# Attention over 48 pairs: one phase of transposes and one of scores per pair, on four shared PSUM banks

## What is computed

```
x + xattn(ctx_1024, layernorm(x), mask, g1, b1, g2, b2, Wq, Wkv, Wout)

xn = layer_norm(ctx, g1, b1)                 # (2, 2048, 512)
ln = layer_norm(latents, g2, b2)             # (2, 128, 512), the latents
q  = ln @ Wq                                 # 16 heads of 64
k, v = split(concat([xn, ln], 1) @ Wkv)
weight = einsum('bhld,bhnd->bhln', q * scale, k * scale)
weight = softmax(where(full_mask, weight, neg), -1)
out = einsum('bhln,bhnd->bhld', weight, v) @ Wout
```

## Time and profile before

| | |
|---|---|
| median of 3 runs | 971.02 us (970.89 to 972.89) |
| the profiled execution | 970.6 us, its span 968.8 us |
| TensorE (PE) busy | 881.1 us, 91% of the span |
| VectorE (DVE) busy | 612.3 us, 63% |
| ScalarE (ACT) busy | 489.1 us, 50% |
| GpSimd (POOL) busy | 313.6 us, 32% |
| the chain that ended last | PE 76%, DVE 12%, ACT 5% |
| the pair loop | from about 52 to 675 us |

### The profile page before, as it was taken

How to read it: one execution, slowest core, us unless ns; L and a number is a source line. 1 busy time by engine, 2 the same in 40 slices (tenths; PEclk the granted TensorE clock), 3 DMA queues, 4 the chain that set the end, 5 groups by cost and what they waited for, 6 DMA issues and landing times.

```text
span 968.8 us, 17165 instructions
## 1 busy us (share of the span) xinstructions
PE 881.1 (91%) x6217; PEld 796.1 (82%) x6217; DVE 612.3 (63%) x1550; ACT 489.1 (50%) x1051; POOL 313.6 (32%) x284
## 2 busy tenths in 40 slices
PE   3799999999999999999999999998686687978997
PEld 2699999999998999999999999887464586867885
DVE  6445556665667776565666566666386377865785
ACT  3465564545555554445464554554557253543553
POOL 3642623120121313131312000220726367744443
PEclk9799999999999999999999999999797888989999
DMA  6255413131323232322212222324220522321320
GB/s 191 59 193 185 157 56 119 66 125 66 111 82 124 87 130 106 124 88 99 83 65 98 87 87 83 124 93 154 95 86 1 190 82 93 131 87 66 110 88 23
DMA packets 45219, 99.13 MB, mean 102 GB/s; under 512 B 3744, under 2 KB 16976, under 8 KB 41936
## 3 DMA queue, kind: packets, MB, share of 16 engines
q1 hardware_dynamic: 45040, 98.00, 29.6%
q10 hardware_dynamic: 96, 0.02, 0.0%
HBM read 88.06 MB, written 8.91 MB: 100 GB/s over the span
## 4 chain that ended last, share of the span: by engine, by line
PE 76%; DVE 12%; ACT 5%; issue 3%; POOL 3%; DMA 1%; DVEq 0%; SPq 0%; ACTq 0%
PE pJ L1620 15%; PE pJ L1622 13%; PE pJ L1621 13%; PE pV L1761 7%; PE pS L1737 7%; PE pT L1747 6%; POOL WS L578 2%; PE pS L1620 2%; DVE KV L1109 2%; PE pS L1621 2%; PE pS L1622 2%; PE pX L1660 1%; DVE late L1577 1%; PE pV L1620 1%; DVE st L1122 1%
## 5 line engine op out<-in xcount | busy, mean ns | idle before, releaser
L1620 PE MATMUL pJ<-WV,XT 128*128 128x256 f32 x544 | 162.9, 300 | 0.0
L1622 PE MATMUL pJ<-WV,XT 128*128 128x256 f32 x544 | 154.3, 284 | 0.0
L1621 PE MATMUL pJ<-WV,XT 128*128 128x256 f32 x544 | 154.2, 284 | 0.0
L1620 PE MATMUL pJ<-XT,WK 128*128 128x384 f32 (+1 forms) x384 | 130.2, 339 | 4.5 <-POOL XT L601 2.6
L1622 PE MATMUL pJ<-XT,WK 128*128 128x384 f32 (+1 forms) x384 | 126.0, 328 | 0.0
L1621 PE MATMUL pJ<-XT,WK 128*128 128x384 f32 (+1 forms) x384 | 125.7, 327 | 0.0
L601 POOL TENSOR_TENSOR XT<-xtmp,XT 128x384 fp32r<-128x384 f32 (+1 forms) x44 | 41.3, 939 | 244.7 <-ACT XT L767 244.4
L842 ACT ACTIVATE PT<-pT 128x384 fp32r<-128x384 f32 x192 | 80.2, 473 | 70.3 <-PE pT L1747 70.3
L1620 PEld LDWEIGHTS pJ<-WV,XT 128*128 128x128 f32 x544 | 104.3, 192 | 10.0 <-issue 8.0
L1109 DVE TENSOR_TENSOR PT<-pT,PT 128x384 fp32r<-128x384 f32 x192 | 95.9, 527 | 18.9 <-ACT PT L842 18.7
L1621 PEld LDWEIGHTS pJ<-WV,XT 128*128 128x128 f32 x544 | 104.4, 192 | 0.0
(11 more groups left out here) (338 smaller groups left out, 2126.2 us busy)
## 6 DMA issues: line engine op xcount, KB each, us to landing
WV<-wv_split SPq DMA_DIRECT2D x20, 1024.0 KB, 4.9
WK<-wk_split SPq DMA_DIRECT2D x40, 512.0 KB, 3.5
xraw<-in_ctx SPq DMA_DIRECT2D x7, 768.0 KB, 4.7
wk_split<-WK SPq DMA_DIRECT2D x8, 512.0 KB, 3.6
wv_split<-WV SPq DMA_DIRECT2D x4, 1024.0 KB, 6.8
wst<-in_L_ffn_Wg SPq DMA_DIRECT2D x4, 1024.0 KB, 5.1
raw<-in_L_ffn_Wu SPq DMA_DIRECT2D x4, 1024.0 KB, 5.1
work<-in_L_ffn_Wd SPq DMA_DIRECT2D x4, 1024.0 KB, 5.3
```

Of the source, the lines that this page charges most:

```text
L1620: te.matmul(dst, a(HI), b(HI), start=start, stop=False)
L1621: te.matmul(dst, a(HI), b(LO), start=False, stop=False)
L1622: return te.matmul(dst, a(LO), b(HI), start=False, stop=stop)
```

## The change

The two phases of transposes of a pair become one at its start, followed by rows_of_scales; the scores of both halves stand side by side behind the value tiles and use the banks of the transposes (BANK: the two of pS and the two of pT), so scores(n, q) wait for the low halves of pair I's probabilities. PT gets a fourth slot (PT3). Keys are projected for pair I + 2, after the outputs, and the third value tiles come behind them. The lists of the other engines follow: key_hi and key_lo move to the end of a pair, joined_hi, value_lo, mask_bias and stats change their places among them, loads, stores and splits of the keys' weights are one pair earlier, and waits that say that a round's context is used up (`after_round`) take its values in.

```diff
             scl = xb("scl", [P, 2, 2, L])
+            PT3 = xb("PT3", [P, 2, CWID], F32R)
...
         ROWS = (slice(0, DH), slice(DH, P))
+        BANK = (pS[:, 0, :], pS[:, 1, :], pT[:, 0, :], pT[:, 1, :])
+        PTS = (PT[:, 0], PT[:, 1], PT[:, 2], PT3)
         pO = pV[:, :].rearrange("p (h s t) -> p h s t", h=2, s=2)
...
-        jobs = ["Q0", "K0.0", "V0.0", "K0.1", "V0.1", "V0.2", "Q1"]
+        jobs = ["Q0", "K0.0", "V0.0", "K0.1", "V0.1", "V0.2", "Q1", "K1.0", "K1.1"]
         for I in range(ITERS):
-            if I + 1 < ITERS:
-                jobs += [f"K{I + 1}.0", f"K{I + 1}.1"]
             if I // 2 + 1 < GROUPS:
                 jobs += [f"V{I // 2 + 1}.{I % 2}"]
+            if I + 2 < ITERS:
+                jobs += [f"K{I + 2}.0", f"K{I + 2}.1"]
             if I + 2 < PAIRS:
...
             return job[f"V{G}.2"] + 1
+
+        def after_round(R):
+            return max(after_keys(PAIRS * R + PAIRS - 1), after_values(PAIRS // 2 * R + PAIRS // 2 - 1))
...
                     keep_wv(0)
-                if I + 1 < PAIRS:
-                    keep_wk(I + 1)
-                if I + 3 < PAIRS:
-                    load_wk(I + 3)
+                    keep_wk(1)
+                    load_wk(3)
+                if I + 2 < PAIRS:
+                    keep_wk(I + 2)
+                if I + 4 < PAIRS:
+                    load_wk(I + 4)
                 if I % 2 == 0 and I // 2 + 1 < 4:
...
                     load_wv(3)
-                if PAIRS <= I + 2 < ITERS:
-                    fetch_wk(I + 2)
+                if PAIRS <= I + 3 < ITERS:
+                    fetch_wk(I + 3)
                 if I % 2 == 0 and 4 <= I // 2 + 2 < GROUPS:
...
             last.then_inc(c_norm, 1)
+            wk_lo(2)
             wq_lo(2)
...
                 C8, C9 = (I + 9) // 4 if (I + 9) % 4 == 0 else 0, (I + 10) // 4 if (I + 10) % 4 == 0 else 0
-                if I + 2 < PAIRS:
-                    wk_lo(I + 2)
+                if I + 3 < PAIRS:
+                    wk_lo(I + 3)
                 if 3 <= C8 < CHUNKS:
...
                 act.wait_ge(c_t, t + 1)
-                if t >= 3:
-                    act.wait_ge(c_o, t - 2)
-                ac.activation(PT[:, t % 3, HI, 0:w], pT[:, t % 2, 0:w], ACT.Copy).then_inc(c_th, 1)
+                if t >= 4:
+                    act.wait_ge(c_o, t - 3)
+                ac.activation(PTS[t % 4][:, HI, 0:w], BANK[t % 4][:, 0:w], ACT.Copy).then_inc(c_th, 1)
...
             query_hi(1)
+            wk_hi(2)
+            key_hi(1, 0)
             wq_hi(2)
+            key_hi(1, 1)
...
                 n, step, G = I + 1, steps_of(I), I // 2 + 1
-                if n < ITERS:
-                    key_hi(n, 0)
-                prob_hi(I, 0, 0)
-                prob_hi(I, 0, 1)
-                if n < ITERS:
-                    key_hi(n, 1)
-                if I + 2 < PAIRS:
-                    wk_hi(I + 2)
+                for h in range(2):
+                    for q in range(2):
+                        prob_hi(I, h, q)
+                scale_rows(I)
                 if I >= 2 and pair_iter(I - 2):
                     joined_hi(I - 2)
-                prob_hi(I, 1, 0)
-                prob_hi(I, 1, 1)
-                scale_rows(I)
                 if step:
...
                     value_hi(G, I % 2)
-                if I + 2 < PAIRS:
-                    query_hi(I + 2)
+                if I + 3 < PAIRS:
+                    wk_hi(I + 3)
                 if n < ITERS:
...
                     x_hi(step[0], step[1] + 1)
+                if I + 2 < ITERS:
+                    key_hi(I + 2, 0)
+                    key_hi(I + 2, 1)
+                if I + 2 < PAIRS:
+                    query_hi(I + 2)
                 if I % 2 == 0 and (I + 4) // 2 < 4:
...
                 dve.wait_ge(c_th, t + 1)
-                low(PT[:, t % 3, LO, 0:w], pT[:, t % 2, 0:w], PT[:, t % 3, HI, 0:w]).then_inc(c_tl, 1)
+                low(PTS[t % 4][:, LO, 0:w], BANK[t % 4][:, 0:w], PTS[t % 4][:, HI, 0:w]).then_inc(c_tl, 1)
...
                 after = mx[:, R, 2 * p + h:2 * p + h + 1] if q == 1 else mid[:, n % 2, h:h + 1]
-                ve.tensor_tensor_reduce(out=SP[:, n % 2, h, c0:c0 + w], in0=pS[:, h, 0:w], in1=MB[:, c0:c0 + w], scale=1.0,
+                ve.tensor_tensor_reduce(out=SP[:, n % 2, h, c0:c0 + w], in0=BANK[2 * q + h][:, 0:w], in1=MB[:, c0:c0 + w], scale=1.0,
                                         scalar=before, op0=ALU.add, op1=ALU.max, accum_out=after).then_inc(c_ttr, 1)
...
             query_lo(1)
+            key_lo(1, 0)
+            key_lo(1, 1)
...
                 C9 = (I + 10) // 4 if (I + 10) % 4 == 0 else 0
-                if n < ITERS:
-                    key_lo(n, 0)
                 prob_lo(I, 0, 0)
...
                 prob_lo(I, 0, 1)
-                if n < ITERS:
-                    key_lo(n, 1)
-                    masked_max(n, 0, 0)
-                    masked_max(n, 0, 1)
                 prob_lo(I, 1, 0)
...
                 if n < ITERS:
-                    masked_max(n, 1, 0)
-                    masked_max(n, 1, 1)
+                    for q in range(2):
+                        for h in range(2):
+                            masked_max(n, q, h)
                     negate(n)
+                if G < GROUPS:
+                    value_lo(G, I % 2)
                 if (I + 2) % PAIRS == 0 and (I + 2) // PAIRS < RNDS:
                     mask_bias((I + 2) // PAIRS)
-                if G < GROUPS:
-                    value_lo(G, I % 2)
-                if I + 2 < PAIRS:
-                    query_lo(I + 2)
                 merge(I)
+                if I + 2 < ITERS:
+                    key_lo(I + 2, 0)
                 if I >= 1 and pair_iter(I - 1):
...
                     stats(C9)
+                if I + 2 < ITERS:
+                    key_lo(I + 2, 1)
+                if I + 2 < PAIRS:
+                    query_lo(I + 2)
                 if I % 2 and G < GROUPS:
...
                     pe.wait_ge(c_jl, job[f"Q{p}"] + 1)
-                if n > 0 or q > 0:
-                    pe.wait_ge(c_ttr, 4 * n + 2 * q)
+                if n > 0:
+                    pe.wait_ge(c_tl, 4 * n - 2 + 2 * q)
                 for o, (qs, ks) in enumerate(((HI, HI), (LO, HI), (HI, LO))):
                     for h, rows in enumerate(ROWS):
-                        last = te.matmul(pS[:, h, 0:w], Q[rows, qs, p, :], KT[rows, q, ks, 0:w], start=o == 0, stop=o == 2)
+                        last = te.matmul(BANK[2 * q + h][:, 0:w], Q[rows, qs, p, :], KT[rows, q, ks, 0:w], start=o == 0, stop=o == 2)
                         if o == 2:
...
                 pe.wait_ge(c_exp, 2 * I + h + 1)
-                if t >= 2:
-                    pe.wait_ge(c_tl, t - 1)
                 for i in range(tiles(I // PAIRS, q)):
-                    last = te.transpose(pT[:, t % 2, P * i:P * i + P], SP[:, I % 2, h, CWID * q + P * i:CWID * q + P * i + P], ident[:, :])
+                    last = te.transpose(BANK[t % 4][:, P * i:P * i + P], SP[:, I % 2, h, CWID * q + P * i:CWID * q + P * i + P], ident[:, :])
                 last.then_inc(c_t, 1)
...
                     for i in range(n):
-                        last = te.matmul(pO[:, h, :, :], VT[:, G % 2, 3 * q + i, 2 * (I % 2) + h, :, :], PT[:, t % 3, :, P * i:P * i + P],
+                        last = te.matmul(pO[:, h, :, :], VT[:, G % 2, 3 * q + i, 2 * (I % 2) + h, :, :], PTS[t % 4][:, :, P * i:P * i + P],
                                          start=q == 0 and i == 0, stop=q == 1 and i == n - 1)
...
             queries(1)
+            project_keys(1, 0)
+            project_keys(1, 1)
...
                 n, step, G = I + 1, steps_of(I), I // 2 + 1
-                if n < ITERS:
-                    project_keys(n, 0)
-                turn_probs(I, 0, 0)
-                turn_probs(I, 0, 1)
-                if n < ITERS:
-                    project_keys(n, 1)
-                    scores(n, 0)
-                else:
-                    pe.wait_ge(c_ttr, 4 * ITERS)
-                    pe.wait_ge(c_ol, PAIRS)
-                    weight_ready(0)
-                    rows(pJ[:, 0, :], OT, 0, 0, 0, True, False)
-                outputs(I, 0)
-                turn_probs(I, 1, 0)
-                turn_probs(I, 1, 1)
+                for h in range(2):
+                    for q in range(2):
+                        turn_probs(I, h, q)
                 rows_of_scales(I)
...
                     x_turn(step[0], step[1])
+                if G < GROUPS:
+                    project_value(G, I % 2, ts[1])
                 if n < ITERS:
+                    scores(n, 0)
                     scores(n, 1)
...
                     rows(pJ[:, 0, :], OT, 0, 1, 4, False, True).then_inc(s_y, 1)
-                if G < GROUPS:
-                    project_value(G, I % 2, ts[1])
+                outputs(I, 0)
+                outputs(I, 1)
+                if step:
+                    x_turn(step[0], step[1] + 1)
```

(17 more changed lines are left out.)

## The result

The changed kernel took **985.6 us** (median of 4 runs, 984.4 to 987.1), the kernel before, run beside it on the same chip, 972.0: a ratio of 1.014 (95% interval 1.012 to 1.016). The change costs 13.6 us. The forecast was 979, its range 966 to 988. The profiled execution took 984.95 us.

A forecast was written before the change was run, and what follows sets the result against it. The prediction took TensorE, nearly always busy at full clock in the pair loop, as the bound. It summed 970.6 + 26.9 + 6.0 - 17.9 - 6.4 = 979.2 and forecast 979 us, range 966 to 988.

The forecast's parts named there:

- The reciprocal: TensorE waits for DVE's reciprocal behind the joined transposes in 16 pairs of rounds 2 and 5: 26.9 us more.
- A plain wait: One reciprocal wait without a late start: chain of 2.22 us against transposes of 1.08, 1.14 us each, 18.2 in 16 pairs.
- The late starts: Extra reciprocal wait where ACT or DVE is still behind (stats, mask_bias, x_hi, split_hi): 8.7 us together.
- Rival B: Faster than before: only plain reciprocal waits are real, late starts and third-value-tile waits are not; about 965, chance 0.13.
- V.2: Third value tiles, now behind the keys, wait for the bank of K.0 until key_lo(I+2,0) is done: 6.0 us more.
- "rest, some 0.7": Remainder of the bank-wait term outside rounds 2 and 5 and the x_hi pairs of 1 and 4: some 0.7 us.
- The scores: Score visits side by side, one instead of two in each of 47 pairs, 0.38 us a visit: 17.9 us saved.
- The four parts of the price: Extra start distances on TensorE in a score visit: 0.09 + 0.10 + 0.08 + 0.10, about 0.38 us.
- Rivals C and E: C: joins pay the second pair's 0.10 us, 984, chance 0.18; E: side-by-side scores save nothing, 997, chance 0.03.
- the clock: TensorE's clock after loop waits: rows show 1.00 through waits up to 1.7 us, none longer; no term in the sum.
- rival D: Each of 26 or so waits 0.4 us dearer, or TensorE's clock falls after a 3 us wait; 990, chance 0.09.
- removed waits: TensorE's waits for KT and for the last pair's exponentials go, as keys are projected a pair further ahead: 6.4 us saved.

The follow-up runs named there:

- e11_split_hi_early_lo_late: Changed kernel with ACT's split_hi(0) and (1) ahead of the exponentials and POOL's split_lo(0) and (1) one pair later; 981.8 us, ratio 1.009.
- e5_v2_before_keys: Changed kernel with the third value tiles ahead of the next keys on odd pairs, on TensorE, ACT and DVE alike; 982.4 us, ratio 1.009.
- e3_split_scores: Changed kernel with the second value tile between scores(n,0) and scores(n,1), so two score visits a pair again; 992.2 us, ratio 1.021.
- e2_sums_early: Changed kernel with DVE's sums moved to the end of the pair before, behind key_lo(I+2,0); 958.3 us, ratio 0.987.
- e8_rows_later: Changed kernel with rows_of_scales behind the first value tile, on TensorE only; 972.2 us, ratio 1.000.
- e9_sums_keys_loads: Kernel of e2_sums_early with ACT's first key_hi ahead of the second x_hi, and load_block(3) and xres load behind OF's last move; 951.2 us, ratio 0.979.
- e4_split_hi_early: Changed kernel with ACT's split_hi(0) and split_hi(1) ahead of exps(n,0) instead of ending I = 42 and 44; 986.5 us, ratio 1.015.

## Why the forecast was right, and where it fell short

**Direction and place were right.** The kernel is slower, by TensorE's waits for linv and by V.2's, and the time behind the loop stayed. The forecast's own markers are there: 16 waits of linv, longest 3.3; V.2's some 6 us; no scores waiting for KT.

**The reciprocal, 26.9 against 27.25.** A plain wait is 1.18 us (forecast 1.14, hence 18.9 instead of 18.2 for 16). The late starts by pair, 17, 19, 21, 23, 43, 45: forecast 0.2, 2.2, 0.8, 2.0, 1.75, 1.75; measured 0.08, 2.12, 0.88, 1.74, 1.75, 1.74. Rival B, that these are not real, falls. `e11_split_hi_early_lo_late` took the two of 1.75 away by moving what they were put down to.

**V.2, 6.0 against 6.08.** Round 2: 0.93 and 1.06 in the x pairs (1.05 each), 0.26 in the others (0.3); rounds 1 and 4: 0.56, 0.38, 0.49, 0.39 (0.5). The "rest, some 0.7" was 1.2, in three Q jobs of round 0. The profiled view of one:
```profile
354.83 0.28 PE L1633 MATMUL pJ<-XT,WK 128*128 128x256 f32 x1
356.01 0.39 PE L1631 MATMUL pJ<-WV,XT 128*128 128x256 f32 x1 [0.90 <-DVE KT L1119]
```

**The scores, 17.9 against 17.7.** The four parts of the price in the prediction add up to 0.37 us, not 0.38; over 47 visits that is 0.5 us. The join is smooth: in a visit of twelve the second tile starts 0.63 us after the first, and the whole takes 1.24, as forecast (1.25).
```profile
60.25 0.79 PE L1748 MATMUL pS<-KT,Q 64*128 64x384 f32 x6
60.88 0.69 PE L1748 MATMUL pT<-KT,Q 64*128 64x384 f32 x6
61.49 1.71 PE L1770 MATMUL pV<-PT,VT 128*128 128x256 f32 x12
```
The pair at the join starts 0.17 us after the one before it, like any third pair. Rivals C and E fall. By the rule of the Trainium skill, "TensorE: Matmul & The Clock Gate", Part 3, the join would have cost 0.10 more each; the trace disagrees here as it did for the third pair of before.

**The step that failed is the clock**, the part of rival D to which I gave too little. The prediction saw that no wait of before was longer than 1.7 us and that some of the new ones would be about 3, and then put the fall at nothing in the sum. It happened behind three of the four waits of 2.9 to 3.3 us (19, 43, 45; not 23): 22, 15 and 11 value matmuls started 0.21 us apart, which with the transposes of scales makes 5.6 us. With the 0.3 of the transposes behind the waits, 979.2 + 5.6 + 0.3 = 985.1; the other differences, 0.4 of waits and 0.2 of scores more, 0.4 of removed waits and 0.7 behind the loop less, and a loop that began 0.25 us later, give 984.9 for the profiled 984.95. The longer chains, D's other half, weren't there. That rival C's number, 984, lies next to the measured 985.6 is luck: what it put the time down to, the join, cost nothing.

**What stays open** is when the clock falls. In the profiled executions of `e5_v2_before_keys` and `e11_split_hi_early_lo_late` it fell behind pair 21, a wait of 2.1 us, and behind pair 23, 2.9 us, at both of which the changed kernel kept it; in the former it stayed up at pair 45, 2.9 us, where the changed kernel's fell. In that of `e3_split_scores` it fell behind pair 19 alone and stayed up at 43 and 45 (2.9 us each). In the kernels whose longest wait in the loop is 1.9 us or less (before, `e2_sums_early`, `e8_rows_later`, `e9_sums_keys_loads`) it never fell. Over all profiled executions of this study it fell behind 17 of the 24 waits of 2.0 to 3.3 us. The length alone doesn't decide.

## What to carry to other kernels

An instruction that waits for a short chain on other engines must be costed by its place on both: what stands ahead of it hides the chain, and what stands ahead of the producer in its own queue lengthens it, down to the last projection's low half. When such a wait is found, look at the producer as well as the waiter; here moving the one brought 31 us and the other 14, since 9.3 us of waits stayed and the waiter shared a bank with what followed (9.6 us). And a wait of two or three microseconds on a busy TensorE should be priced with a chance of slow starts behind it; here they came behind most such waits and cost 1.0 to 2.6 us each time.

## What the hardware showed that I had not expected

**The lower clock after short waits**: starts of 256 columns 0.21 us apart instead of 0.12, 11 to 22 value matmuls at a time in the changed kernel, behind waits of 2.1 to 3.3 us over all kernels, some of them and not others; granted clock 0.64 to 0.87 over the windows of three such waits shown above, 1.00 over that of pair 23. The Trainium skill, "TensorE: Matmul & The Clock Gate", section "HAM oscillation — how this bites in real kernels", describes a fall of the clock in the wait between two bursts of matmuls, so that the next burst starts slow; the trace agrees that this happens.

**DVE beside POOL** (`e4_split_hi_early`): three instructions with SBUF inputs alone took 0.9 to 1.1 us instead of 0.2 to 0.4 while POOL subtracted two tiles from SBUF, a fourth, the second multiply, 0.49 instead of 0.43, and those that read PSUM (0.68 for 512 columns) their usual time. The Trainium skill, "SBUF — State Buffer", section "Who interferes with whom", says that a DVE instruction with two SBUF inputs contends with a GpSimd instruction that reads SBUF, and that the ports they share are an exclusive lock; the first multiply and the join agree with it. The negation has one SBUF input of two columns and was held up as well; the section lists its operation, tensor_scalar, among those that can contend under conditions, which no run here tests.

**A small DMA behind large ones**: DVE waited 4.8 us for the last move of OF (two of 32 KB) with 2.5 MB requested from 5.8 us ahead of it on SP's queue, 3.6 with them from 7.9 us ahead, and 3.0 with 1 MB ahead and the rest behind it.
